# Row maxima of a decoder layer kept as fp16 and turned by an fp16 identity

## The chip, the cores and the metric

The kernel runs on one NeuronCore of a Trainium2 chip. The metric is the device time of one execution in microseconds (us), and of several executions their median. TensorE (PE) does the matmuls and the transposes, VectorE (DVE), ScalarE (ACT) and GpSimd (POOL) the elementwise work, and all transfers are issued by SyncE (SP).

## The reference

One decoder layer on x of 8 batches x 128 positions x 512 features, in three blocks, each `x = x + block(layernorm(x))`:

- **Self-attention**: 128 heads. A head's score is a 4-wide content product plus a 64-wide product of `x @ Wq_rope` with a key that all heads share, divided by sqrt(68), then softmax over 128 keys, then 4-wide values, then `@ Wo`.
- **Cross attention** on `ctx_4096`: 32 query heads of width 16, 8 key/value heads, rotary angles from `itok_BxS2_0_2047`, softmax, `@ Wo`.
- **Feed-forward**: a 512x512 linear layer with bias, plus 8 low-rank experts of rank 16, of which a gate picks two for each token.

Softmax here needs a row maximum for each query and head. Any number near the maximum will do, since the same number stands in numerator and denominator.

## The kernel before

Nearly all products are made from fp16 pairs (high part and rest), so one fp32-like product is three fp16 matmuls of 512 columns.

**The loop** runs over 32 groups g of 4 heads (`step(g, par)` on each engine; the first two and the last three steps are spelled out, the others are looped two at a time). On PE a step has two halves t = 0 and 1, and each half has eight slots n. Slot n holds three matmuls of the rope projection of group g (`project`, L1200). Slots 1 to 4 also hold the rough scores (`rough_scores`, L1236, four matmuls of 128 columns for a batch). DVE reduces these to negated row maxima (`row_max`, L795) in the tile `mneg`, a [128, 16] block for each half: 4 heads x 4 batches. Slots 3 to 6 hold the exact scores of the group before (`scores`, L1266 and L1268). Slot 7 holds two things one right after the other: `max_turn` (L1244), which turns one `mneg` block to [16, 128] in PSUM bank 6, and `weigh` (L1283), twelve matmuls that multiply probabilities and values, each on a strip of 32 columns of the array. After `max_turn`, DVE scales the block and writes it as fp16 (`max_out`, L888, tile `mT`), and SP sends it by DMA into a row of `QC`, where the exact scores of the next half take it in as one more contraction row.

There are two halves in each step, so `max_turn` runs 64 times. In `transpose(out, in_, identity)` the data is the stationary operand (here 16 columns) and the 128-column identity streams through.

**The tail** is one pipeline over 32 units u (8 batches x 4 groups of heads) of the cross attention, with the projections, the layer norms and the feed-forward of the batches woven in between. In each unit PE turns queries and keys (`turn`, L1370), makes rough scores (`x_rough`, L1380, on strips of 64 rows), turns the maxima of the unit (`x_max_turn`, L1388, a [128, 8] block of the tile `xm`), makes the exact scores of the unit before (`x_scores`, L1397, strips of 64 rows), weighs (`x_weigh`, L1411, strips of 32 columns) and turns back (`x_back`, L1418). ACT copies the turned maxima out (`x_max_out`, L713) and SP sends them into a row of `KQ`.

The order on each engine is written out by hand, and engines meet at semaphores only. The identity `ident` is fp32; a second one, `id16`, is cast to fp16 by POOL after the loop (L530), in a tile of the tail that lies over tiles of the loop. PSUM bank 0 is also seen as fp16 (`PT16`), and `turn` writes there.

Of the kernel before, what the change touches and what calls it, by code (L numbers as in the profile page):

```python
# [7 lines left out]
F16 = mybir.dt.float16  # L8
I32 = mybir.dt.int32
ALU = mybir.AluOpType  # L10
ACT = mybir.ActivationFunctionType
AX = mybir.AxisListType

P = 128
B, S, DM = 8, 128, 512
# [8 lines left out]
GH = 4  # L24
# [6 lines left out]
MS = 16.0  # L31
PSC = 64.0
ATT_SCALE = float(HD + RD) ** -0.5
# [4 lines left out]
REP = XH // NKV  # L38
# [7 lines left out]
UQ, UC = XT_H // 2, XT_H // 2 + XT_H // REP  # L46
# [9 lines left out]
def build(nc, x, ctxT, pos, wdkr, wup, wqr, wo, xwq, xwkv, xwo, bw, ag, lb, bb, out):  # L56
    es = ExitStack()
    with es:
        def sem(name):
            return es.enter_context(nc.semaphore(name))  # L60
# [5 lines left out]
        def sb(name, shape, dt=F32):  # L66
            n = size[dt]
            for s in shape[1:]:
                n *= s
            at = top[0]  # L70
            top[0] = at + (n + 63) // 64 * 64
            return nc.alloc_sbuf_tensor_at(name, shape, dt, offset=at)

        xs = sb("xs", [P, B, DM])
        ident = sb("ident", [P, P])
# [28 lines left out]
        turns = sb("turns", [P, B, HF])  # L104
        red = sb("red", [P, 2, B, HF])
        sincos = sb("sincos", [P, 2, B, HF])
        cosq = sb("cosq", [P, B, HF])
        sinq = sb("sinq", [P, B, 2, HF])
        cosk = sb("cosk", [P, B, HF])
# [20 lines left out]
        Vg = sb("Vg", [P, 2, 2, B, 32], F16)  # L130
        os_at = top[0]
        OS = sb("OS", [P, 2, GH * S])
        mneg = sb("mneg", [P, 2, 2, GH, B // 2])
        mT = sb("mT", [16, 2, S], F16)
        end1 = top[0] + 4 * KT * TOK * 2
        top[0] = pr_at
# [36 lines left out]
        id16 = sb("id16", [P, P], F16)  # L173
# [6 lines left out]
        qr = sb("qr", [P, DM])  # L180
        KQ = sb("KQ", [P, 4, UC, S], F16)
        xvz = sb("xvz", [P, B, NKV, 32])
        xm = sb("xm", [P, 2, 2 * REP])
        xmT = sb("xmT", [2 * REP, 2, S], F16)
        XPT = sb("XPT", [P, 2, 2, REP * S])
        OW = sb("OW", [P, 2 * S])
# [15 lines left out]
        PS = es.enter_context(nc.psum_tensor("PS", [P, 8, 512], F32))  # L202

        PT16 = PS[:, 0, :].bitcast(F16)


        YD = nc.dram_tensor("q_content_parts", [H, CR, TOK], F16, kind="Internal").ap()
# [5 lines left out]
        s_zero, s_id = sem("zeroed"), sem("ident_ready")  # L213
# [12 lines left out]
        s_a, s_m, s_mt, s_me = sem("a_ready"), sem("max_ready"), sem("mT_ready"), sem("mT_out")  # L226
# [25 lines left out]
        s_xmt, s_xme, s_xmd = sem("xmax_turned"), sem("xmax_out"), [sem("xmax_in0"), sem("xmax_in1")]  # L252
# [10 lines left out]
        bQ, bA, bB, bM, bO = (0, 1), (2, 3), (4, 5), 6, 7  # L263
# [42 lines left out]
        def g_is(g, n):  # L306

            return isinstance(g, int) and g == n
# [134 lines left out]
        def _(pool):  # L443
            nc.gpsimd.memset(ident[:], 0.0).then_inc(s_pch, 1)
            pool.wait_ge(s_pch, 1)
            nc.gpsimd.affine_select(out=ident[:], in_=ident[:], compare_op=ALU.not_equal, fill=1.0,
                                    base=0, pattern=[[-1, P]], channel_multiplier=1).then_inc(s_id, 1)
            nc.gpsimd.memset(power[:], -0.5)
            nc.gpsimd.memset(xv[:, :, :, XD_], 1.0)
            nc.gpsimd.memset(wscale[:], WS)  # L450
# [95 lines left out]
            for u in range(FIRST, LAST):  # L546
                b, r = (u + 1) // KT, (u + 1) % KT
# [4 lines left out]
                if r == 1 and 0 <= b + 1 < B:  # L552
# [5 lines left out]
                    q, t = (w.rearrange("p (h d) -> p h d", d=XD_) for w in (qr[:], rt[:, 0]))  # L558
# [25 lines left out]
        def _(act):  # L584
# [123 lines left out]
            def x_max_out(u):  # L708
                if 0 <= u < NU:
                    act.wait_ge(s_xmt, u + 1)  # L710
                    if u >= 2:
                        act.wait_ge(s_xmd[u % 2], 32 * (u // 2))
                    nc.scalar.activation(xmT[:, u % 2, :], PS[0:2 * REP, 0, 3 * S:], ACT.Copy, scale=1 / MS).then_inc(s_xme, 1)  # L713

            def x_exps(u, h):
                if 0 <= u < NU:
# [5 lines left out]
            def turned_out(u):  # L722
                if 0 <= u + 2 < NU:
                    v = u + 2
                    act.wait_ge(s_xt, v + 1)
                    if v >= 4:
                        act.wait_ge(s_st, 2 * (v - 3))
                    nc.scalar.activation(KQ[:, v % 4].rearrange("p c s -> p (c s)"), PT16[:, 0:UC * S], ACT.Copy).then_inc(s_kq, 1)

            for u in range(FIRST, LAST):  # L730
                b, r = (u + 1) // KT, (u + 1) % KT
# [25 lines left out]
                if r == 3:  # L757
                    norm_high(1, b + 2, bF[0], s_xq)
                x_max_out(u + 1)
                x_exps(u, 0)  # L760
                if 0 <= u - 1 < NU:
# [7 lines left out]
        def _(dve):  # L769
# [114 lines left out]
            def max_out(g, t):  # L884
                dve.wait_ge(s_mt, 2 * g + t + 1)
                if not isinstance(g, int) or g >= 1:
                    dve.wait_ge(s_md[t], 16 * g)
                nc.vector.tensor_scalar(mT[:, t, :], PS[0:16, bM, 0:S], math.log(PSC) / ATT_SCALE, 1 / MS, ALU.add, ALU.mult).then_inc(s_me, 1)  # L888

            def o_out(g, t):  # L890
                dve.wait_ge(s_pv, 2 * g + t + 1)
# [9 lines left out]
            def step(g, par):  # L901
# [6 lines left out]
                if g_is(g, 1):  # L908
                    max_out(0, 0)
# [8 lines left out]
                if reached(g, 1, 1):  # L918
                    max_out(g - 1, 1)
# [14 lines left out]
                if reached(g, 0):  # L934
                    max_out(g, 0)
# [140 lines left out]
            for u in range(FIRST, LAST):  # L1076
                b, r = (u + 1) // KT, (u + 1) % KT
# [68 lines left out]
        def _(pe):  # L1146
# [91 lines left out]
                last.then_inc(s_a, 1)  # L1238

            def max_turn(g, par, t):  # L1240
                pe.wait_ge(s_m, 8 * g + 4 * t + 4)
                if not isinstance(g, int) or g >= 1 or t >= 1:
                    pe.wait_ge(s_me, 2 * g + t)
                nc.tensor.transpose(PS[0:16, bM, 0:S], mneg[:, par, t].rearrange("p j b -> p (j b)"), ident[:]).then_inc(s_mt, 1)  # L1244

            for b in range(B):
                bank_read("kv", b)
# [39 lines left out]
            def step(g, par):  # L1287
                o = 1 - par
                for t in range(2):
                    for n in range(8):  # L1290
                        if reached(g, 1):
                            project(g, par, 2 * t + n // KT, n % KT)
                        if g_is(g, 1) and t == 0 and n == 0:
                            pe.wait_ge(s_ul, 16)
                            pe.wait_ge(s_vl, B)
                            max_turn(0, 0, 0)
# [15 lines left out]
                        if n == 7:  # L1312
                            if t == 0 and reached(g, 1, 1):
                                max_turn(g - 1, o, 1)
                            if t == 1 and reached(g, 0):
                                max_turn(g, par, 0)
                            if t == 0 and reached(g, 2, 2):
                                weigh(g - 2, par, 1)
                            if t == 1 and reached(g, 1, 1):
                                weigh(g - 1, o, 0)  # L1320
# [36 lines left out]
            def turn(u):  # L1357
# [9 lines left out]
                for c in range(UC):  # L1367
                    src = q[:, (t * UQ + c) * P:(t * UQ + c + 1) * P] if c < UQ else \
                        k[:, (t * (UC - UQ) + c - UQ) * P:(t * (UC - UQ) + c - UQ + 1) * P]
                    last = nc.tensor.transpose(PT16[:, c * S:(c + 1) * S], src, id16[:])  # L1370
                last.then_inc(s_xt, 1)
# [13 lines left out]
            def x_max_turn(u):  # L1385
                pe.wait_ge(s_xm, 2 * u + 2)
                pe.wait_ge(s_kq, min(u + 2, NU))
                nc.tensor.transpose(PS[0:2 * REP, 0, 3 * S:], xm[:, u % 2], ident[:]).then_inc(s_xmt, 1)  # L1388

            def x_scores(u):  # L1390
                pe.wait_ge(s_xmd[u % 2], 32 * (u // 2 + 1))
# [37 lines left out]
            for u in range(FIRST, LAST):  # L1429
                b, r = (u + 1) // KT, (u + 1) % KT  # L1430
# [62 lines left out]
                if 0 <= u + 1 < NU:  # L1493
                    x_max_turn(u + 1)
# [36 lines left out]
```

## Time and profile before

| What | Before |
|---|---|
| median of 3 runs | 869.03 us (868.4 to 870.11) |
| the profiled execution: time, span | 867.85 us, 865.9 us |
| PE busy | 803.9 us (93%) |
| DVE, ACT, POOL busy | 647.9, 568.5, 582.8 us |
| mean granted TensorE clock | 0.978 |

The span goes from the first to the last instruction; the time of an execution is about 2 us longer. Busy times overlap between engines. PE's busy time is modelled from pipelined matmuls, so how far apart two matmuls start says more of their cost than how long one takes.

### The profile page before, as it was taken

Reading aid. Unit: us, or ns where it says so; the run is one execution under the profiler, and the core shown is the slowest. Engines: PE = TensorE matmul, PEld = TensorE weight load, DVE = VectorE, ACT = ScalarE, POOL = GpSimd, SP = SyncE. Lnnn points to the kernel's source line nnn. Section 1 sums busy time; section 2 is a strip of 40 time slices with the busy share of each in tenths; the row PEclk is TensorE's granted clock in tenths of the full one; section 3 lists DMA queues with packets and bytes.
Section 4 is the critical chain, followed back from the end, with each engine's and each line's share of the span. In section 5 each row is a group of like instructions: output and inputs, shape, how many; then the busy total and the mean of one; then the engine's idle time right before and its main releaser. Section 6 shows DMA issues by size and latency. Waiting matters only on the chain.

```text
span 865.9 us, 17867 instructions
## 1 busy us (share of the span) xinstructions
PE 803.9 (93%) x5624; PEld 395.2 (46%) x5624; DVE 647.9 (75%) x1209; ACT 568.5 (66%) x1045; POOL 582.8 (67%) x492
## 2 busy tenths in 40 slices
PE   4999999999999999999999999999848688999986
PEld 3464444444454444444444444444313344555433
DVE  7866777767677888777888767788787567888754
ACT  4757777777777777777777777777530465555641
POOL 7747888888788878888888878885543223333210
PEclk9999999999999999999999999999978799999999
DMA  8344455434334332434333433432130000000001
GB/s 334 110 166 146 92 156 169 139 85 112 101 90 105 85 108 78 107 97 123 85 82 91 113 104 89 109 89 56 29 88 0 1 1 3 15 13 15 13 13 37
DMA packets 51227, 74.69 MB, mean 86 GB/s; under 512 B 9968, under 2 KB 33520, under 8 KB 50672
## 3 DMA queue, kind: packets, MB, share of 16 engines
q1 hardware_dynamic: 51184, 74.18, 30.7%
q8 instruction: 20, 0.33, 0.2%
q14 instruction: 23, 0.19, 0.1%
HBM read 38.16 MB, written 18.87 MB: 66 GB/s over the span
## 4 chain that ended last, share of the span: by engine, by line
PE 84%; DVE 8%; ACT 2%; issue 2%; DMA 1%; SPq 1%; POOL 0%; DVEq 0%; ACTq 0%
PE PS L1200 39%; PE PS L1152 8%; PE PS L1236 7%; PE PS L1266 6%; PE PS L1268 6%; PE PS L1283 5%; PE PS L1411 2%; PE PS L1325 1%; PE PS L1418 1%; PE PS L1380 1%; PE PS L1397 1%; PE PS L1426 1%; PE PS L1456 1%; DVE xm L1027 1%; PE PS L1244 1%
## 5 line engine op out<-in xcount | busy, mean ns | idle before, releaser
L492 POOL TENSOR_TENSOR Pl<-PR,Ph 128x512 f16<-128x512 f32 x254 | 285.8, 1157 | 24.7 <-ACT Ph L668 24.7
L661 ACT ACTIVATE PR<-PS 128x512 f32<-128x512 f32 x256 | 152.6, 597 | 135.0 <-PE PS L1268 128.5
L795 DVE TENSOR_REDUCE mneg<-PS 128x4 f32<-128x512 f32 x256 | 174.6, 684 | 38.2 <-PE PS L1236 34.7
L1200 PE MATMUL PS<-XTh,Wh 128*128 128x512 f16 x512 | 194.5, 380 | 0.0
L1200 PE MATMUL PS<-XTh,Wl 128*128 128x512 f16 x512 | 193.7, 378 | 0.0
L1200 PE MATMUL PS<-XTl,Wh 128*128 128x512 f16 x512 | 193.5, 378 | 0.0
L783 DVE SCALAR_TENSOR_TENSOR QS<-PS,QC 64x512 f16<-64x512 f32 x256 | 175.5, 686 | 18.0 <-ACT QC L593 10.9
L593 ACT ACTIVATE QC<-PS 64x512 f16<-64x512 f32 x256 | 150.7, 589 | 10.6 <-PE PS L1200 4.3
L668 ACT ACTIVATE Ph<-PR 128x512 f16<-128x512 f32 x256 | 139.3, 617 | 0.0
L474 POOL TENSOR_TENSOR Wh<-Wraw,wscale 128x1024 f16<-128x1024 f32 x32 | 60.6, 1893 | 70.8 <-PE PS L1200 67.5
L1236 PEld LDWEIGHTS PS<-KC,QC 112*128 112x128 f16 x1024 | 78.8, 97 | 62.2 <-issue 2.7
L1236 PE MATMUL PS<-KC,QC 112*128 112x128 f16 x1024 | 99.3, 219 | 0.0
L1266 PE MATMUL PS<-QC,KC 113*128 113x512 f16 x256 | 97.7, 381 | 0.0
L1268 PE MATMUL PS<-QS,KS 128*128 128x512 f16 x256 | 97.2, 380 | 0.0
L1200 PEld LDWEIGHTS PS<-XTh,Wh 128*128 128x128 f16 x512 | 49.9, 97 | 64.9 <-issue 25.9
L543 POOL TENSOR_TENSOR rstd<-rstd,power 128x1 f32<-128x1 f32 x16 | 8.8, 550 | 103.1 <-DVE rstd L1006 103.1
L1200 PEld LDWEIGHTS PS<-XTh,Wl 128*128 128x128 f16 x512 | 49.5, 97 | 61.3
L888 DVE TENSOR_SCALAR mT<-PS 16x128 f16<-16x128 f32 x64 | 17.8, 279 | 77.3 <-PE PS L1244 77.3
L480 POOL TENSOR_TENSOR Wl<-Wraw,Wh 128x1024 f16<-128x1024 f32 x32 | 68.2, 2131 | 2.5
L1200 PEld LDWEIGHTS PS<-XTl,Wh 128*128 128x128 f16 x512 | 49.6, 97 | 38.9
L478 POOL TENSOR_TENSOR Wraw<-Wraw,wscale 128x1024 f32<-128x1024 f32 x32 | 60.6, 1893 | 0.2
L1325 PE MATMUL PS<-wo_sb,U 128*128 128x512 f32 x64 | 35.7, 696 | 13.6 <-DVE U L962 12.3
(213 smaller groups left out, 1163.4 us busy)
## 6 DMA issues: line engine op xcount, KB each, us to landing
Wraw<-in_wqr SPq DMA_DIRECT2D x32, 512.0 KB, 4.6
QS<-QC SPq DMA_DIRECT2D x64, 256.0 KB, 3.2
head_outputs<-OS SPq DMA_DIRECT2D x256, 40.0 KB
q_content_parts<-stg SPq DMA_DIRECT2D x12, 256.0 KB, 2.8
k_content_parts<-stg SPq DMA_DIRECT2D x12, 256.0 KB, 3.1
QC<-q_content_parts SPq DMA_DIRECT2D x128, 24.0 KB
KC<-k_content_parts SPq DMA_DIRECT2D x32, 96.0 KB
xs<-in_x SPq DMA_DIRECT2D x8, 256.0 KB, 4.5
```

What stands on the lines that cost most here:

```text
L480: nc.gpsimd.tensor_tensor(Wl[:, par], Wraw[:, par], Wh[:, par], ALU.subtract).then_inc(s_ws, 1)
L492: nc.gpsimd.tensor_tensor(Pl[:, b], PR[:, b % 4], Ph[:, b], ALU.subtract).then_inc(s_pl, 1)
L593: nc.scalar.activation(QC[0:RD, par, t, 2 * p + h, :], PS[RD * h:RD * (h + 1), bQ[c % 2], :], ACT.Copy, scale=1 / WS).then_inc(s_qh, 1)
L661: nc.scalar.activation(PR[:, b % 4, :], PS[:, bB[b % 2], :], ACT.Exp, scale=ATT_SCALE).then_inc(s_e, 1)
L668: nc.scalar.activation(Ph[:, b, :], PR[:, b % 4, :], ACT.Copy).then_inc(s_ph, 1)
L783: nc.vector.scalar_tensor_tensor(QS[0:RD, par, t, j, :], PS[RD * h:RD * (h + 1), bQ[c % 2], :], 1 / WS, QC[0:RD, par, t, j, :], ALU.mult, ...
L795: nc.vector.tensor_reduce(mneg[:, par, b // 4, :, b % 4], PS[:, bA[b % 2], :].rearrange("p (j k) -> p j k", j=GH), AX.X, ALU.max, negate=T ...
L1152: last = mm(PS[:, bank, 0:c1 - c0], xt[:, k], wt[:, k, c0:c1], start=(start and k == 0 and n == 0), stop=(stop and k == KT - 1 and n == 2))
L1200: last = mm(PS[:, bQ[c % 2], :], wt[:, par, k, p * P:(p + 1) * P], xt[:, k, sl], start=(k == 0 and n == 0), stop=(k == KT - 1 and n == 2))
L1236: last = mm(PS[:, bA[b % 2], j * S:(j + 1) * S], QC[0:MROW, par, b // 4, j, b % 4 * S:(b % 4 + 1) * S], KC[0:MROW, par, b * S:(b + 1) * S] ...
L1266: mm(PS[:, bB[b % 2], :].rearrange("p (j q) -> p j q", j=GH), KC[0:MROW + 1, par, b * S:(b + 1) * S], QC[0:MROW + 1, par, t, :, b % 4 * S: ...
L1268: mm(PS[:, bB[b % 2], :].rearrange("p (j q) -> p j q", j=GH), KS[:, b * S:(b + 1) * S], QS[:, par, t, :, b % 4 * S:(b % 4 + 1) * S], start ...
```

## The change

The tiles `mneg` and `xm` become fp16, so the two reductions of DVE write fp16. The two transposes that turn them take an fp16 identity and write fp16 into PSUM. In the loop that identity is a new one, `id16l`, cast by POOL at the start of the kernel and placed in the bytes of `sincos`, which ACT first writes after the loop; in the tail it is `id16`. The two instructions that read the turned maxima (L888, L713) read fp16.

```
+id16l = sincos[:].rearrange("p a b f -> p (a b f)").bitcast(F16)[:, 0:P]
-mneg = sb("mneg", [P, 2, 2, GH, B // 2])
+mneg = sb("mneg", [P, 2, 2, GH, B // 2], F16)
-xm = sb("xm", [P, 2, 2 * REP])
+xm = sb("xm", [P, 2, 2 * REP], F16)
 PT16 = PS[:, 0, :].bitcast(F16)
+PM16 = PS[:, 6, :].bitcast(F16)
...
# POOL, after the affine_select that makes ident
+pool.wait_ge(s_id, 1)
+nc.gpsimd.tensor_copy(id16l, ident[:]).then_inc(s_id, 1)
...
# ACT, x_max_out
-nc.scalar.activation(xmT[:, u % 2, :], PS[0:2 * REP, 0, 3 * S:], ACT.Copy, scale=1 / MS).then_inc(s_xme, 1)
+nc.scalar.activation(xmT[:, u % 2, :], PT16[0:2 * REP, UC * S:(UC + 1) * S], ACT.Copy, scale=1 / MS).then_inc(s_xme, 1)
...
# DVE, max_out
-nc.vector.tensor_scalar(mT[:, t, :], PS[0:16, bM, 0:S], ...)
+nc.vector.tensor_scalar(mT[:, t, :], PM16[0:16, 0:S], ...)
...
# PE, max_turn
+if g_is(g, 0):
+    pe.wait_ge(s_id, 2)
-nc.tensor.transpose(PS[0:16, bM, 0:S], mneg[:, par, t].rearrange("p j b -> p (j b)"), ident[:]).then_inc(s_mt, 1)
+nc.tensor.transpose(PM16[0:16, 0:S], mneg[:, par, t].rearrange("p j b -> p (j b)"), id16l).then_inc(s_mt, 1)
...
# PE, x_max_turn
-nc.tensor.transpose(PS[0:2 * REP, 0, 3 * S:], xm[:, u % 2], ident[:]).then_inc(s_xmt, 1)
+nc.tensor.transpose(PT16[0:2 * REP, UC * S:(UC + 1) * S], xm[:, u % 2], id16[:]).then_inc(s_xmt, 1)
```

## Rows read from the trace of the kernel before

**Rows 1.** Busy time and clock by stretch (us from the span's start).

```profile
core 0: us, PE busy (x) PEld busy (x) DVE busy (x) ACT busy (x) POOL busy (x), PEclk, DMA share, GB/s
100.00:600.00 500.00, 500.00 (x3463) 241.10 (x3462) 383.08 (x610) 382.12 (x683) 426.49 (x339) 1.00 0.40 104
650.00:697.00 47.00, 36.67 (x184) 16.41 (x183) 29.50 (x59) 12.60 (x22) 14.02 (x18) 0.77 0.00 1
697.00:835.00 138.00, 127.33 (x1157) 66.51 (x1155) 107.93 (x300) 79.68 (x172) 44.93 (x50) 0.99 0.03 10
```

**Rows 2.** Who waited for whom in the loop, 62 to 615 us.

```profile
DVE mT L888 <- PE PS L1244: 75.9, 63, 1.5
POOL Wh L474 <- PE PS L1200: 67.5, 29, 2.5
```

**Rows 3.** PE in order of time, the first turn of the loop (start, length).

```profile
62.41 0.27 PE L1244 MATMUL PS<-ident,mneg 128*16 128x128 f32 x1 [1.40 <-DVE mneg L795]
62.52 0.38 PE L1200 MATMUL PS<-XTh,Wh 128*128 128x512 f16 x1
```

**Rows 4.** PE in order of time, later: two turns, and rough scores between them.

```profile
403.37 0.38 PE L1200 MATMUL PS<-XTh,Wl 128*128 128x512 f16 x1
403.58 0.27 PE L1244 MATMUL PS<-ident,mneg 128*16 128x128 f32 x1
403.78 0.62 PE L1283 MATMUL PS<-Ph,Vg 128*32 128x512 f16 x8
...
405.85 0.39 PE L1236 MATMUL PS<-KC,QC 112*128 112x128 f16 x4
406.08 0.38 PE L1200 MATMUL PS<-XTh,Wh 128*128 128x512 f16 x1
...
412.39 0.27 PE L1244 MATMUL PS<-ident,mneg 128*16 128x128 f32 x1
```

**Rows 5.** PE in order of time, one unit of the tail.

```profile
757.01 0.38 PE L1152 MATMUL PS<-Wxh,Al 128*128 128x512 f16 x1
757.32 0.40 PE L1380 MATMUL PS<-KQ 48*128 48x128 f16 x8
757.65 0.27 PE L1388 MATMUL PS<-ident,xm 128*8 128x128 f32 x1
757.86 0.39 PE L1397 MATMUL PS<-KQ 49*128 49x256 f16 x4
```

**Rows 6.** The chain that ended last: 60 to 617 us by line, then pieces of the tail.

```profile
by line: PE PS L1200 58.7%; PE PS L1236 10.2%; PE PS L1266 9.9%; PE PS L1268 9.9%; PE PS L1283 8.4%; PE PS L1244 1.3%; PE PS L1325 1.0%; issue 0.3%; DVE V L827 0.1%; DVE mneg L795 0.1%; DVE stg L822 0.1%; ACT V L648 0.1%
...
674.60 4.40 PE PS L1152 x12
679.34 0.22 PE PS L1388
...
686.05 0.30 PE PS L1388
...
707.62 2.59 PE PS L1152 x12
...
833.69 0.11 PE PS L1388
```

**Rows 7.** POOL and DVE in order of time at the start, and the cast after the loop.

```profile
8.95 1.04 POOL L468 TENSOR_TENSOR rstd<-rstd,power 128x4 f32<-128x4 f32 x1
...
10.78 3.73 DVE L834 TENSOR_SCALAR xn<-xs,mv,rstd 128x512 f32<-128x512 f32 x8
...
630.24 0.29 POOL L530 CAST id<-ident 128x128 f16<-128x128 f32 x1 [2.12 <-PE PS L1283]
```

**Rows 8.** Groups by line and shape: busy us, mean ns.

```profile
L1244 PE MATMUL PS<-ident,mneg 128*16 128x128 f32 x64 | 17.4, 273 | 1.4 <-DVE mneg L795 1.4
L795 DVE TENSOR_REDUCE mneg<-PS 128x4 f32<-128x512 f32 x256 | 174.6, 684 | 38.2 <-PE PS L1236 34.7
L899 DVE TENSOR_TENSOR Pl<-PR,Ph 128x512 f16<-128x512 f32 x2 | 1.6, 859 | 0.0
```

More of the change, by code:

```diff
@@ L887, in max_out @@
                     dve.wait_ge(s_md[t], 16 * g)
-                nc.vector.tensor_scalar(mT[:, t, :], PS[0:16, bM, 0:S], math.log(PSC) / ATT_SCALE, 1 / MS, ALU.add, ALU.mult).then_inc(s_me, 1)
+                nc.vector.tensor_scalar(mT[:, t, :], PM16[0:16, 0:S], math.log(PSC) / ATT_SCALE, 1 / MS, ALU.add, ALU.mult).then_inc(s_me, 1)
             def o_out(g, t):
```

## The prediction

> **What bounds the kernel now.** I read first the busy time by stretch, then the waits of the loop, then the chain that ended last, and last PE's instructions one by one.
>
> Between 100 and 600 us PE is busy all 500 us, at a granted clock of 1.00 [rows 1]. That is the loop, and in it others wait for PE: DVE's `max_out` waits for the turned maxima 63 times, 75.9 us in all, and POOL waits 67.5 us for PE before it may overwrite weights [rows 2]. The chain says the same: from 60 to 617 us nearly all of it is PE, and L1244 is 1.3% of it [rows 6]. 1.3% of 557 us is 7.2 us, or 0.11 us for each of 64. So in the loop an instruction that leaves PE 0.05 us earlier makes the kernel 0.05 us shorter, as long as no other engine fills up. DVE, ACT and POOL are busy 77, 76 and 85% there [rows 1].
>
> From 697 to 835 us PE is busy 127 of 138 us [rows 1], so the tail is bound by PE too, but less fully: the chain goes through DVE and ACT now and then. Of 32 `x_max_turn` 26 lie on it, from 679.34 to 833.69 us [rows 6]. From 650 to 697 us the clock is 0.77: part of this stretch runs at 1.2 GHz, the lower level [rows 1].
>
> **What the turns cost, and will cost.** The length of a matmul (273 ns) holds pipeline time that overlaps its neighbours, so I price by how far starts lie apart.
>
> *The fp32 turn.* The first of the loop has no `weigh` behind it: it starts at 62.41 and the next matmul at 62.52, so 128 columns of fp32 take 0.11 us [rows 3]. In the later ones `weigh` follows, and the distance is 0.20 us (403.58 to 403.78) [rows 4]. The other 0.09 us are the step from the whole array to strips. The tail shows that step beside fp16 alone: an fp16 matmul of 512 columns, which elsewhere starts 0.21 us before the next (403.37 to 403.58) [rows 4], is followed 0.31 us later when strips come (757.01 to 757.32) [rows 5]. `x_max_turn`, between two kinds of strips, is 0.21 us ahead of its follower (757.65 to 757.86) [rows 5]: again 0.11 and 0.1. The change keeps every such step, so only the 0.11 can shrink.
>
> *The fp16 turn* isn't in this trace with 16 columns. Nearest is `rough_scores`: four fp16 matmuls of 128 columns each take 0.23 us (405.85 to 406.08), 0.057 each [rows 4]. It could be nothing below that (128 columns must stream), and at worst 0.11, what fp32 takes. I take 0.057, since the columns that stream and their type are the same; the stationary block is narrower and loads in no more time. The saving is 0.11 - 0.057 = 0.053 us a turn.
>
> On the step to strips the Trainium skill, TensorEngine Tiling, Key Properties, has the rule that a change of tiling mode drains TensorE. By that rule, the 0.09 stays whatever the type: the trace agrees with its 0.09 to 0.10 us behind fp32 and behind fp16.
>
> *Loop:* 64 x 0.053 = 3.4 us, all on the chain [rows 6, 8].
>
> *Tail:* 26 turns on the chain. Two of them (the one at 686.05 and the next) ran at the lower clock, where a turn with its step took 0.30 in place of 0.20 [rows 6]; there the saving doubles to 0.106. 24 x 0.053 + 2 x 0.106 = 1.5 us. The other 6 lie beside a longer path through ACT and DVE, and save nothing.
>
> **The rest of the change.**
>
> *POOL's cast at the start.* The same cast after the loop took 0.29 us [rows 7]. It comes ahead of a row of memsets, which end just before 8.95 us, when POOL makes the first half of `rstd`. That takes 1.04 us, to 9.99, and DVE uses it at 10.78 [rows 7]. So 0.29 plus a semaphore step of about 0.05 are covered by 0.79 us. Without this cover they would cost 0.35. The new wait of PE comes at its first turn, at 62 us; nothing is queued behind a semaphore that was raised some 60 us before.
>
> *DVE's reduction writing fp16.* 684 ns with fp32 out [rows 8]. The dearest DVE row that takes 512 fp32 to fp16 is L899 with 859 ns; the cheapest outcome is no change. Four reductions a half-step would add up to 4 x 0.175 = 0.7 us to DVE, which idles 23% [rows 1] of a half-step of 8.8 us (403.58 to 412.39, one turn to the next [rows 4]), 2.0 us. I take 0; the 0.7 would be hidden too.
>
> *The two readers.* They read 128 fp16 in place of fp32, no more elements than before. DVE waited for nearly every turned block [rows 2], and each comes earlier now. If an fp16 read were slower by as much as the read takes, some 0.3 us, `mT` would be late by that; the exact scores need it over 1 us after and the chain never stopped for it in the loop [rows 6]. No DMA is added, moved or resized, and SP's queue keeps its order.
>
> **Sum.** -3.4 - 1.5 = -4.9 us. The profiled execution took 867.85 us (span 865.9), which would become 862.95. It was 1.2 us below the median of the runs, 869.03; against the median the forecast is 864.1 us, 0.56% faster.
>
> **Rivals.**
>
> *Only the loop pays* (12%): the tail's chain goes back and forth between PE, ACT and DVE; what PE saves in a unit could be waited away at DVE. For it: DVE is busy 108 of 138 us there [rows 1]. Against it: 26 of 32 turns on the chain. 869.0 - 3.4 = 865.6 us.
>
> *A floor* (6%): what I read as 0.11 plus 0.09 is a fixed 0.20 us that `weigh` needs between its predecessor and itself (its three waits, its weight loads). Then the change doesn't do what it says: 869 us. Against it: in rows 3 the turn takes 0.11, and behind 512 columns the step adds 0.1 and isn't swallowed by 0.2 of streaming.
>
> *One more drain in each turn* (4%, the other side): an fp16 block of 16 columns may be put into a strip of its own kind, with one step of 0.094 us before it and one behind. In the loop that is 64 x (0.094 - 0.053) = +2.6 us, less 1.5 in the tail, where steps surround the turn anyway: +1.1, 870.1 us. It decides from an added 0.077 us a turn (4.9 / 64). If instead the strip is `weigh`'s own kind, the step only moves ahead of the turn and the forecast stands. For the possibility the Trainium skill, TensorEngine Tiling, Restrictions and Gotchas, says that column tiling excludes transposes of fp32 input only; fp16 is free to be tiled. That moves no number here.
>
> *The clock comes back later* (3%): behind the loop PE idles and falls to 1.2 GHz, and from 650 to 697 us it goes between the levels. Twelve matmuls of 512 columns, mostly at the lower level, took 4.40 us against 2.59 [rows 6]. Everything arrives 3.4 us earlier, and the clock may come back at another point of the work. A unit with twelve such matmuls, wholly at the lower level, would cost up to 2.6 us more for them and as much for the rest; to turn -4.9 into +1.8 takes 6.7 us, one and a half such units: 870.8 us. A small shift of 1 us either way is likely and in my range.
>
> *More than forecast* (2%): fp32 by several passes. If the turn took four, fp16 would save 3/4 of the whole 0.20, 0.15 us: 64 x 0.15 + 26 x 0.15 = 13.5 us, 855.5 us. Against it: rows 3, where the whole turn takes 0.11. Beside it stands the Trainium skill, FP8 and Floating Point Precision, TensorE Precision Notes: true fp32 is four passes through the array. The trace disagrees for transposes: 0.11 is about two of the fp16 price.
>
> **How the numbers follow.** The forecast has 73%, the rivals 12, 6, 4, 3 and 2. The likeliest's own ends: at best 0.11 - 0.053 (128 columns at the full rate of rows 4, 0.21 / 4) for all 96 turns, 64 x 0.057 + 32 x 0.057, is -5.6; at worst 0.045 for 88 turns is -4.0. With 1 us for the clock's point of return and 1 us for the spread of the runs (868.4 to 870.11) that is 861.5 to 867; to take in the loop alone with its spread I end at 867.3. About 0.2%, 1.7 us, is what a measurement of this kernel can tell from no change. Faster: 73 + 12 + 2, less 2 for spread, 0.85. Within: 6 + 4 + 3 and 0.12 in sum. Slower: 0.03.
>
> **What would show it.** In the profile after, the turn followed by `project` starts about 0.055 us before it, and one followed by `weigh` about 0.15 before; two turns in the loop lie 8.75 us apart, not 8.81; L795 still takes 684 ns; `weigh` starts no later relative to the turn. A drain ahead of the turn would show as 0.31 us in place of 0.21 from the last `project` matmul. If the loop is 3.4 us shorter and the total isn't 4 to 6, the loss is in the clock row from 610 to 700 us. Wrong would be: the distance of 0.20 unchanged, or a wait of PE on DVE inside the loop.

## The result, and the profile after

| | Before | After |
|---|---|---|
| median, first comparison (6 runs each) | 868.71 us | 862.34 us |
| ratio, 95% interval | | 0.993 (0.9908 to 0.9953) |
| profiled execution: time, span | 867.85, 865.9 us | 860.44, 858.5 us |
| PE busy | 803.9 us | 796.8 us |
| DVE, ACT, POOL busy | 647.9, 568.5, 582.8 us | 641.3, 568.0, 583.0 us |

The change makes the kernel 0.7% faster in this comparison, 0.4% (0.9942 to 0.9975) in a second and 0.7% (0.9909 to 0.9955) in a third (below). The mean over all 23 runs of the changed kernel is 863.3 us, over 52 runs of the kernel before that stood beside them 868.2: 4.8 us less, with an interval of 0.8 us either way if all runs are taken as one sample. By comparison the means differ by 6.0, 3.9 and 5.3 us. The forecast was 4.9 less.

The first view is PE in order of time, for the first turn of the loop. It answers to [rows 3].

```profile
62.23 0.22 PE L1250 MATMUL PS<-sincos,mneg 128*16 128x128 f16 x1 [1.40 <-DVE mneg L799]
62.38 0.39 PE L1204 MATMUL PS<-XTh,Wh 128*128 128x512 f16 x1
```

The fp16 turn (now L1250; the identity lies in `sincos`) is 0.15 us ahead of the next matmul of the whole array, where fp32 was 0.11 ahead. Taken alone that is slower. The next rows, the same view of two later turns, answer to [rows 4].

```profile
400.85 0.38 PE L1204 MATMUL PS<-XTh,Wl 128*128 128x512 f16 x1
401.16 0.22 PE L1250 MATMUL PS<-sincos,mneg 128*16 128x128 f16 x1
401.17 0.65 PE L1289 MATMUL PS<-Ph,Vg 128*32 128x512 f16 x8
...
409.90 0.22 PE L1250 MATMUL PS<-sincos,mneg 128*16 128x128 f16 x1
```

Before, the turn stood 0.21 us behind `project`'s last matmul and 0.20 ahead of `weigh`. Now it stands 0.31 behind and 0.01 ahead. So the step from the whole array to strips has moved ahead of the turn: the fp16 turn with its 16 columns runs in a strip of 32, like the weighing matmuls, and the other strips start to weigh while the turn still streams in the first (the rows of double16 below show the strips apart). From one turn to the next it is 8.74 us, where it was 8.81 [rows 4].

The busy time by stretch answers to [rows 1], with the same columns.

```profile
100.00:600.00 500.00, 500.00 (x3491) 242.17 (x3489) 381.27 (x616) 385.02 (x688) 430.17 (x342) 1.00 0.41 104
650.00:697.00 47.00, 36.61 (x240) 17.66 (x240) 30.47 (x65) 17.48 (x32) 14.28 (x16) 0.85 0.00 1
697.00:835.00 138.00, 127.92 (x1135) 67.13 (x1138) 105.97 (x303) 76.40 (x168) 44.55 (x51) 0.98 0.03 11
```

The loop is still all PE at the higher level of the clock. Who waited for whom in the loop (62 to 615 us: us in total, times, longest) answers to [rows 2].

```profile
PE PS L1250 <- DVE mneg L799: 1.4, 1, 1.4
DVE mT L892 <- PE PS L1250: 79.3, 64, 1.5
POOL Wh L478 <- PE PS L1204: 63.9, 29, 2.5
```

In this profile there is no new wait: PE waits for DVE at the first turn only, as before, and the others still wait for PE. The groups answer to [rows 8], and one is new, the reader of the turned block: first as it was before (L888), then as it is now (L892).

```profile
L888 DVE TENSOR_SCALAR mT<-PS 16x128 f16<-16x128 f32 x64 | 17.8, 279 | 77.3 <-PE PS L1244 77.3
L799 DVE TENSOR_REDUCE mneg<-PS 128x4 f16<-128x512 f32 x256 | 172.1, 685 | 36.8 <-PE PS L1240 34.6
L892 DVE TENSOR_SCALAR mT<-PS 16x128 f16<-16x128 f16 x64 | 13.6, 212 | 79.3 <-PE PS L1250 79.3
```

The reduction takes 685 ns with fp16 out, where it took 684. The reader fell from 279 to 212 ns, off the chain. At the start, POOL and DVE in order of time answer to [rows 7].

```profile
1.61 0.29 POOL L451 CAST sincos<-ident 128x128 f16<-128x128 f32 x1
...
9.30 1.04 POOL L472 TENSOR_TENSOR rstd<-rstd,power 128x4 f32<-128x4 f32 x1
...
10.60 3.74 DVE L838 TENSOR_SCALAR xn<-xs,mv,rstd 128x512 f32<-128x512 f32 x8
```

The new cast pushed POOL's first `rstd` from 8.95 to 9.30 us, the 0.35 that the prediction had for it. It ends at 10.34, and DVE wanted it at 10.60.

In the tail, PE in order of time for one unit answers to [rows 5].

```profile
750.22 0.38 PE L1156 MATMUL PS<-Wxh,Al 128*128 128x512 f16 x1
750.53 0.40 PE L1386 MATMUL PS<-KQ 48*128 48x128 f16 x8
750.86 0.22 PE L1394 MATMUL PS<-id,xm 128*8 128x128 f16 x1
751.01 0.39 PE L1403 MATMUL PS<-KQ 49*128 49x256 f16 x4
```

Here the turn has other strips on both sides, so both steps stay, and its distance to the next falls from 0.21 to 0.15.

Where the time went, by stretches between turns, worked out from the starts of all turns in each profile (us; the last row is the steady part of the tail, from its turn 11 to its turn 27):

| Stretch | Before | After | Difference |
|---|---|---|---|
| start to first turn of the loop | 62.4 | 62.2 | -0.2 |
| first to last turn of the loop | 554.0 | 550.2 | -3.9 |
| to the first turn of the tail | 62.8 | 59.8 | -3.1 |
| first to last turn of the tail | 154.3 | 154.0 | -0.2 |
| to the end | 32.4 | 32.3 | 0.0 |
| sixteen units of the tail | 83.9 | 83.2 | -0.65 |

The loop gave 3.9 us against 3.4 forecast. The 3.1 us between loop and tail are none of the change's terms, and the tail as a whole gave less than its steady part. Both had to be explained.

### The profile page after: what moved, and what is told of

The parts are those of the page before. It is cut to its first block, busy times and chain, and to the rows that moved or that the text cites. A ratio compares the mean times of both kernels' runs of the same rounds, so it can differ in the third digit from the quotient of the medians.

```text
span 858.5 us, 17869 instructions
## 1 busy us (share of the span) xinstructions
PE 796.8 (93%) x5624; PEld 393.2 (46%) x5624; DVE 641.3 (75%) x1209; ACT 568.0 (66%) x1045; POOL 583.0 (68%) x493
## 4 chain that ended last, share of the span: by engine, by line
PE 83%; DVE 9%; ACT 2%; issue 2%; SPq 1%; DMA 1%; POOL 0%; DVEq 0%; ACTq 0%
PE PS L1204 39%; PE PS L1156 8%; PE PS L1240 7%; PE PS L1272 6%; PE PS L1274 6%; PE PS L1289 5%; PE PS L1417 2%; PE PS L1424 1%; PE PS L1250 1%; PE PS L1386 1%; PE PS L1403 1%; PE PS L1432 1%; PE PS L1331 1%; PE PS L1462 1%; DVE xm L1031 1%
## 5 line engine op out<-in xcount | busy, mean ns | idle before, releaser
L799 DVE TENSOR_REDUCE mneg<-PS 128x4 f16<-128x512 f32 x256 | 172.1, 685 | 36.8 <-PE PS L1240 34.6
L478 POOL TENSOR_TENSOR Wh<-Wraw,wscale 128x1024 f16<-128x1024 f32 x32 | 60.6, 1893 | 67.1 <-PE PS L1204 63.9
L892 DVE TENSOR_SCALAR mT<-PS 16x128 f16<-16x128 f16 x64 | 13.6, 212 | 79.3 <-PE PS L1250 79.3
L482 POOL TENSOR_TENSOR Wraw<-Wraw,wscale 128x1024 f32<-128x1024 f32 x32 | 60.6, 1895 | 0.2
```

What stands on the lines that cost most here:

```text
L799: nc.vector.tensor_reduce(mneg[:, par, b // 4, :, b % 4], PS[:, bA[b % 2], :].rearrange("p (j k) -> p j k", j=GH), AX.X, ALU.max, negate=T ...
```

## Experiments

Time ratios are to the kernel before on the same chip, with 95% intervals. "Loop" is from the first to the last turn of the loop, "sixteen units" is the steady part of the tail as above, both in us from each kernel's profile.

| Kernel | Median, us | Ratio | Loop | Sixteen units |
|---|---|---|---|---|
| before | 868.0 to 868.9 | | 554.0 | 83.9 |
| after_again | 864.27 | 0.9958 (0.9942 to 0.9975) | 550.7 | 83.25 |
| loop_only | 864.95 | 0.9962 (0.9947 to 0.9977) | 550.15 | 83.9 |
| tail_only | 868.06 | 0.9994 (0.9979 to 1.0009) | 554.05 | 83.24 |
| wide128 | 863.68 | 0.9949 (0.9928 to 0.997) | 550.8 | 83.25 |
| double32 | 875.39 | 1.0065 (1.0039 to 1.0091) | 560.8 | 83.9 |
| double16 | 867.27 | 0.9979 (0.9961 to 0.9997) | 553.55 | 83.24 |
| beside | 866.23 | 0.9956 (0.9935 to 0.9977) | 550.0 | 82.3 |
| beside_ow | 860.35 | 0.9903 (0.9879 to 0.9928) | 550.0 | 80.6 |
| after_third | 862.3 | 0.9932 (0.9909 to 0.9955) | 550.7 | 83.2 |
| ow_first | 866.75 | 0.9976 (0.9956 to 0.9996) | 550.1 | 83.2 |
| beside_ow2 | 859.49 | 0.9888 (0.9864 to 0.9912) | 550.0 | 80.6 |

**The same kernel again: after_again and after_third.** No edit.

> The changed kernel once more. Theory A (the two terms of the sum are all there is): PE's starts in the profile give 3.9 us for the loop and 1.5 for the tail, so 5.4 us below before, ratio 0.9938. Theory B (the medians' 6.4 us hold something more, a clock that comes back at a better point of the work behind the loop): 6 us or more again, ratio 0.993 or lower, and the stretch from the last turn of the loop to the first of the tail is again about 3 us shorter in its profile. If it was luck of one execution, that stretch is within 1 us of before.

Measured: 0.9958, a smaller gain than either theory said; A's 0.9938 lies just below the interval, B's 0.993 farther out. The stretch between loop and tail took 60.6 us, 2.2 less than before.

> The changed kernel again, beside the two below. The distances of PE say 3.9 us for the loop and 1.4 for the tail: ratio 0.994 to the kernel before.

Measured: 0.9932, and 59.8 us for that stretch. The two comparisons and the first don't quite agree. One reason is that the stretches in which PE idles vary from execution to execution. Over all thirteen profiles the stretch from the start to the first turn took from 62.0 to 64.5 us and the stretch between loop and tail from 59.8 to 63.2, with no order by kind of kernel: the fp32 loops have 62.8 (before), 60.3 (tail_only) and 62.4 (double32), the fp16 loops 59.8, 60.6 and 59.8 (the changed kernel three times), 63.2 (loop_only), 62.1 (wide128), 61.5 (double16), 62.3 (beside and beside_ow2), 60.3 (beside_ow) and 60.1 (ow_first). Loop_only is the one that speaks against B most: its loop is the changed one, and its stretch is the longest of all. With the mean over all runs 4.8 us lower, no more than A needs, B falls; the 3.1 us of the first profile belong mostly to one execution.

A second reason is the clock, by the mean granted clock that is on record for every run. In the second comparison the ten runs of the changed kernel have 0.9749 on average and the 28 of the kernel before 0.9775; in the third it is 0.9766 and 0.9769. Among the runs of the kernel before alone, a clock lower by 0.001 goes with 0.5, 0.6 and 0.7 us more in the three sets of them that have clocks on record (the ten runs of after_again lie within 0.002 and show no such order). So 1.3 us or more of what the second comparison lacks is an estimate of the clock's share: 3.9 and 1.3 make 5.2, and the third, where the clocks are alike, has 5.3 by its means, both near theory A's 5.4. Whether the lower clock of the second comparison has to do with the change stays open; the third speaks against it.

A third, smaller reason is a wait in the loop that the first profile doesn't have. Both later profiles of the changed kernel have this row for PE between 63 and 600 us:

```profile
PE PS L1272 <- DMA QC<-mT: 0.5, 1, 0.5
```

Once, at 134.7 and at 136.1 us, the exact scores waited half a microsecond for the turned maxima to land in `QC`. The distance between turns that holds the wait is 0.69 and 0.65 us longer than the others, and so these two loops took 550.7 us where the same loop took 550.0 in beside and beside_ow. The other eight profiles with an fp16 loop and the three with an fp32 loop have no such row, so it isn't shown that the change brings it.

**One part at a time: loop_only and tail_only.** Each has only the edits of its part; the other stays as before.

> Only the 64 turns of the loop are fp16, the 32 of the tail stay fp32. Theory A: -3.9 us (63 distances of 0.061 us), ratio 0.9955. Theory B: the loop's gain plus about 1 us or more for the clock, -5 us, ratio 0.994.

> Only the 32 turns of the tail are fp16. Theory A: -1.5 us, ratio 0.998, units 0.06 us shorter in three of four. Theory that the tail swallows the gain (DVE and ACT on its chain): 0, ratio 1.000. Theory B has nothing to add here, since all before the tail stands where it stood.

Measured: the loop alone gives 3.3 us (0.9962), and its profile has the loop at 550.15 us. The tail alone can't be told from no change by time, and the clock (0.9757 on average against 0.9775) was against it here too. By the trace of the steady part it can: sixteen units take 83.24 us where before and loop_only have 83.9. That is 0.65 us, twelve turns of 0.054: in each four units, three are 0.05 to 0.06 us shorter and one, whose turn lies beside the path through ACT and DVE, is not (5.40, 4.96, 6.26, 4.36 us before; 5.34, 4.90, 6.20, 4.37 after). So the steady part doesn't swallow the gain. For the whole tail, 26 turns at 0.054 would be 1.4 us, but that is an estimate: from the first to the last turn of the tail tail_only took 153.9 us against 154.25, only 0.3 less. Its first ten units were 0.45 us longer than before, in a part where the clock changes its level at other places in every profile.

**Out of the strip: wide128.** The block of maxima is padded to 128 columns, so the turn takes the whole array.

```
-mneg = sb("mneg", [P, 2, 2, GH, B // 2], F16)
+mwide = nc.alloc_sbuf_tensor_at("mneg", [P, 2, 2, 128], F16, offset=free_at)   # over cosq to sink
+mneg = mwide[:, :, :, 0:GH * B // 2].rearrange("p a t (j b) -> p a t j b", j=GH)
...
-nc.tensor.transpose(PM16[0:16, 0:S], mneg[:, par, t].rearrange("p j b -> p (j b)"), id16l)
+nc.tensor.transpose(PM16[0:128, 0:S], mwide[:, par, t], id16l)
```

> The changed kernel, but each turned block of the loop is padded with zeros from 16 to 128 columns (16 are used), so the turn can't go into a strip of 32 columns. If the gain comes from fp16 columns streaming in half the time, the step to strips moves back behind the turn (0.21 us ahead of the turn, 0.15 behind it) and the time stays within 0.5 us of the changed kernel. If it comes from the turn sharing the strips of the weighing matmuls, most of the loop's 3.9 us is lost again.

PE in order of time, two turns of wide128:

```profile
401.83 0.38 PE L1207 MATMUL PS<-XTh,Wl 128*128 128x512 f16 x1
402.05 0.22 PE L1253 MATMUL PS<-sincos,mneg 128*128 128x128 f16 x1
402.20 0.61 PE L1292 MATMUL PS<-Ph,Vg 128*32 128x512 f16 x8
...
410.80 0.22 PE L1253 MATMUL PS<-sincos,mneg 128*128 128x128 f16 x1
```

The same view of its first turn, which no `weigh` follows:

```profile
62.90 0.22 PE L1253 MATMUL PS<-sincos,mneg 128*128 128x128 f16 x1 [1.40 <-DVE mneg L802]
62.96 0.38 PE L1207 MATMUL PS<-XTh,Wh 128*128 128x512 f16 x1
```

This is what the prediction had drawn: 0.06 us ahead of `project`, and in the later turns 0.22 behind, 0.15 ahead, and 8.75 us from turn to turn, 0.054 less than before (with a digit more, 8.807 and 8.753). The kernel with the strip has 8.737. So of 0.070 us a turn 0.054 come from the type and 0.016 from sharing the strips with `weigh`. Over the whole loop the strip is worth only 0.6 us more (550.2 against 550.8) where 0.016 for each of 61 distances would be 1.0: the two turns with no `weigh` behind them have a step of their own on either side (0.31 and 0.15 against 0.21 and 0.06), 0.25 us together, and one distance of the first profile was 0.15 longer than the rest. By time the two kernels can't be told apart. The Trainium skill, TensorEngine Tiling, Restrictions and Gotchas, lists transposes with fp32 input among what column tiling excludes; by that rule only the fp16 turn may enter a strip, and the three kernels agree: fp32 with 16 columns stays outside, fp16 with 16 goes in, fp16 with 128 can't.

**What one turn costs: double32 and double16.** Each has the turn of the loop issued twice.

```
+nc.tensor.transpose(PS[0:16, bM, 0:S], mneg[:, par, t].rearrange("p j b -> p (j b)"), ident[:])
 nc.tensor.transpose(PS[0:16, bM, 0:S], mneg[:, par, t].rearrange("p j b -> p (j b)"), ident[:]).then_inc(s_mt, 1)
```

> The kernel before with each of the 64 fp32 turns of the loop made twice into the same place (the first has no reader). My price for one fp32 turn without the step to strips is 0.107 us: +6.8 us, ratio 1.008. If the 0.20 us between turn and weighing were a fixed floor, the second turn would hide in it: 0.

> The changed kernel with each of the 64 fp16 turns of the loop made twice into the same place. If an fp16 turn costs its 128 columns, 0.054 to 0.057 us: +3.5 us against the changed kernel, so about 2 us below before. If it overlaps with the three other strips and costs nothing: 0 against the changed kernel.

PE in order of time, double32:

```profile
408.80 0.38 PE L1200 MATMUL PS<-XTh,Wl 128*128 128x512 f16 x1
409.01 0.27 PE L1244 MATMUL PS<-ident,mneg 128*16 128x128 f32 x1
409.12 0.27 PE L1245 MATMUL PS<-ident,mneg 128*16 128x128 f32 x1
409.32 0.62 PE L1284 MATMUL PS<-Ph,Vg 128*32 128x512 f16 x8
```

The second fp32 turn adds its 0.11 us and the step behind stays 0.20: no fixed floor. The loop grew from 554.0 to 560.8 us, 6.7 us for 63 distances, 0.107 each, and the time by 6.5 us.

PE in order of time, double16:

```profile
404.66 0.38 PE L1204 MATMUL PS<-XTh,Wl 128*128 128x512 f16 x1
404.96 0.22 PE L1250 MATMUL PS<-sincos,mneg 128*16 128x128 f16 x1
404.98 0.40 PE L1290 MATMUL PS<-Ph,Vg 128*32 128x512 f16 x3
405.02 0.22 PE L1251 MATMUL PS<-sincos,mneg 128*16 128x128 f16 x1
405.08 0.59 PE L1290 MATMUL PS<-Ph,Vg 128*32 128x512 f16 x5
```

Three weighing matmuls, one for each other strip, are recorded as started at 404.98, although both turns stand ahead of them in the program; the second turn starts at 405.02 in the first strip. Still the loop grew from 550.2 to 553.55 us, 0.053 to 0.056 for each, and the time was 1.6 us below the kernel before where 2 were expected. So the overlap with the other strips doesn't hide a turn. The reading of the order is that the first strip has all its passes to do after the turns, and the step back to the whole array waits for it.

**Beyond the change: the turn of the tail beside the weighing.** An fp16 block fits in a strip, so in the tail the turn may join `x_weigh` and spare two steps a unit.

```
 # PE, each unit (beside, beside_ow)
-x_max_turn(u + 1)
 x_scores(u)
+x_max_turn(u + 1)
 x_weigh(u - 1)
...
 # ACT, each unit (ow_first, beside_ow)
+copy of OW
 x_exps(u, 0)
-copy of OW
 x_exps(u, 1)
```

> The changed kernel with the tail's turn moved on PE from between rough and exact scores (both in strips of 64 rows) to right ahead of the weighing matmuls (strips of 32 columns, where an fp16 block of 8 columns fits). That takes two steps between kinds of strips out of each unit, 0.19 us of PE. If PE's order sets the tail: 26 x 0.19 = up to -4.9 us against the changed kernel. If ACT sets it (its copy of the maxima now comes 0.2 us later, ahead of the exp and of the copy OW that the chain goes through): the gain is lost, 0 to -1 us, in the units where ACT's OW lies on the chain.

> As the kernel with the turn beside the weighing, and ACT copies OW ahead of both exps. If ACT's order took the gain away, it comes back in part: x_back can start 0.15 us earlier, -2 to -4 us against the changed kernel. If the queries and keys' copy behind the exps then comes too late for the rough scores, it is slower than the variant without this.

> The changed kernel with ACT's copy OW ahead of both exps, the tail's turn where it was. If the gain of the variant with both edits is ACT's order alone: all of it, -2.66 us over sixteen units of the steady tail. If it needs the moved turn: the copy now waits for the end of the weighing (0.2 us later than with the turn moved), so x_back starts hardly earlier, and the steady tail is within 0.5 us of 83.2.

> Both edits again: sixteen units of the steady tail 80.6 us, the whole 4 us below the changed kernel in this same call (2.7 us for these sixteen units, the rest for the others).

`beside` alone: 1 us off the sixteen units, not the 2.3 of 12 x 0.19. PE in order of time in one of these units shows what took its place, and the last row, from the table of waits, adds it up over the steady part (722 to 805 us: us in total, times, longest).

```profile
789.39 0.39 PE L1403 MATMUL PS<-KQ 49*128 49x256 f16 x4
789.71 0.22 PE L1394 MATMUL PS<-id,xm 128*8 128x128 f16 x1
789.72 0.64 PE L1417 MATMUL PS<-XPT,xvz 128*32 128x256 f32 x8
...
791.02 0.44 PE L1424 MATMUL PS<-ident,OW 128*128 128x128 f32 x2 [0.16 <-ACT OW L769]
...
PE PS L1424 <- ACT OW L769: 2.0, 12, 0.2
```

In twelve of the sixteen units PE reaches the turn back (L1424) earlier and waits 0.16 us for ACT's copy `OW`, which stands behind an exp. The changed kernel has no such wait there. With the copy ahead of the exps (`beside_ow`) the sixteen units take 80.6 us, 2.65 less than after. The copy's place alone (`ow_first`) gives nothing there, 83.2, so the gain needs both edits. The chain of the changed kernel, and then of `beside_ow2`, around the 24th turn of the tail (start, length):

```profile
787.64 0.15 PE PS L1394
787.79 0.33 PE PS L1403 x4
788.12 0.61 PE PS L1417 x8
788.73 0.02 issue
788.75 0.39 ACT OW L769
789.15 0.04 issue
789.19 0.44 PE PS L1424 x2
```

```profile
787.15 0.22 PE PS L1403 x4
787.37 0.15 PE PS L1394
787.52 0.43 PE PS L1417 x8
787.95 0.02 issue
787.97 0.49 PE PS L1376 x6
788.46 0.01 issue
788.48 0.44 PE PS L1424 x2
```

In the changed kernel ACT's copy lies on the chain. In `beside_ow2` the copy is gone from it, and PE's own work (L1376) leads to the turn back. Side by side the medians are 859.49 us and 862.30 for the changed kernel, 2.8 us less where 4 were expected (3.8 by the means, with about 2 us either way), and in both comparisons this version lies 1% below the kernel before (0.9903 and 0.9888).

`beside` and `ow_first` came out slower than the changed kernel in time although their sixteen units are shorter or as short. Their runs have a mean granted clock of 0.968 to 0.972 in 7 of 12 and 8 of 12 cases, where all 23 of the changed kernel were at 0.974 to 0.98. Busy time and clock by stretch near the end, `beside` and then the changed kernel:

```profile
830.00:850.00 20.00, 16.11 (x76) 6.95 (x77) 8.07 (x30) 3.71 (x9) 1.82 (x2) 0.74 0.08 28
```

```profile
824.00:844.00 20.00, 15.58 (x104) 7.32 (x103) 10.83 (x42) 5.66 (x14) 1.81 (x2) 1.00 0.07 28
```

In `beside` the clock fell to 1.2 GHz twice in this stretch, and it took 36.8 us from the last turn of the tail to the end in place of 32.3. `ow_first` fell twice too (0.86 from 808 to 820 us, 0.83 from 840 to 850): 157.8 us from its first to its last turn of the tail in place of 154.0, and 34.0 to the end. Not every such fall comes with these two edits: after_third and tail_only have one each (0.83 from 830 to 840 us) and took 34.0 and 33.9 us to the end. In the 7 us before the first fall of `beside`, at 830.8 us, PE had waited 0.67 us for OW twice and 1.05 us for the DMA of the maxima. That such waits bring the clock down is argued from this, not shown: one and the same kernel fell in one of its three profiles (after_third) and not in the others, and `beside_ow` and `beside_ow2` have no fall here.

## Why the prediction was right, point by point

- **PE sets the loop.** Right. Loop_only and the doubled fp32 turns moved the time as their loops moved, within the noise: 3.3 us for 3.9, 6.5 for 6.7. The prediction's "the chain never stopped" for `mT` held with one exception of 0.5 us in each of two of the three profiles of the changed kernel.
- **An fp32 turn is 0.11 us, the rest of the 0.20 is the step to strips.** Right, by double32 (0.107) and wide128, where the step of 0.09 stands behind the turn as drawn.
- **An fp16 turn is 0.057 us, the saving 0.053.** Right for the type alone (wide128: 0.054). In the changed kernel the saving was 0.070 in a steady half-step, because the turn shares strips with `weigh`. The prediction had no term for that. The term of the loop, 3.4 us, measured 3.9 in the first profile and 3.3 in the other two, which hold the wait of 0.5; a little of the extra is lost again at the two turns that no `weigh` follows.
- **Where the step stands.** The text foresaw that it could move ahead of the turn, and said that then the forecast stands. It did, but the signs given in "What would show it" were for the other case: the turn before `project` starts 0.15 us ahead of it, not 0.055, and the one before `weigh` 0.01, not 0.15. The mark of a drain ahead (0.31 in place of 0.21) is what appeared. The rival of one more drain in each turn fell: there is one into strips and one out of them, as before.
- **26 turns of the tail pay, 1.5 us.** Right by the trace in the steady part (12 of 16, 0.054 each, 0.65 us). The 1.4 us for all 26 are worked out from that and not measured, and time doesn't prove them.
- **Costs at nothing.** The cast was covered with 0.26 us left; the reduction took 685 ns; the reader got faster, 212 ns.
- **The clock's point of return moves the time by 1 us either way.** Right in kind and too small: two kernels (beside, ow_first) came out some 4 us above what their work says. Their clocks are 0.004 below those of the runs beside them, which at 0.6 to 0.7 us for each 0.001 is an estimate of 2.5 to 3 of the 4. Single profiles of like kernels differ by 3.4 us in the stretch between loop and tail.
- **The sum.** -4.9 us; over all runs -4.8. That they agree to 0.1 us is luck: the strip's share (0.5 us) was not in the sum, the clock took some back in one comparison, and the single comparisons gave 6.0, 3.9 and 5.3. The first one's 6.4 us by the medians holds 3.1 us from the stretch between loop and tail in its profile, which no term has.
- **The range.** Its best end is added up a little wrong: 96 x 0.057 is 5.5 us, and 5.6 only with the two turns at the lower clock counted twice. It changes nothing.

## What to carry to other kernels

Price a matmul by how far starts lie apart, and look for one place where it has no change of strips behind it: one row gave 0.11 us where 64 others gave 0.20, and only the 0.11 could shrink. A transpose made fp16 may also change in which part of the array it runs; put it next to work of the same strips (worth 2.65 us over sixteen units here, together with moving the copy that then stood in the way). Differences of 1 to 3 us in a program whose PE idles for stretches need many runs and a look at the mean granted clock of both sides, or the distances inside the trace where the clock is full, which repeat to 0.01 us.

## What the runs showed of the hardware

- An fp16 transpose with 16 stationary columns runs in a strip of 32 columns with a step ahead of it (0.31 us behind a matmul of 512 columns) and 0.01 us ahead of matmuls in such strips; with 8 columns it stands 0.01 ahead of them too (beside). The same with fp32 and 16 columns, or with fp16 and 128, starts 0.21 us behind, with the step after it (0.20 and 0.15 to the next).
- Issued twice, an fp32 transpose of 128 moving columns adds 0.107 us and an fp16 one 0.053 to 0.056 (double32, double16).
- After the turn in the first strip, matmuls of the other strips start 0.01 us later, and the trace shows them started ahead of a second turn that stands before them in the program.
- DVE's `tensor_scalar` of 16 x 128 elements out of PSUM took 212 ns with fp16 in, 279 ns with fp32 in.
